# Expert weights of the fourth network: the split of all ten pieces moved ahead of the first chunk's mean, and cut in two parts

## The reference, cut to what matters

```
h = x @ W_in + b_in
for l in range(3):
    agg = segment_sum(h[src], dst) / deg
    logits = concat([h, agg]) @ router_W[l] + router_b[l]
    gates = softmax of the two largest logits, 0 elsewhere
    weak   = relu(agg @ weak_W[l]   + weak_b[l])          # 4 experts, 256 -> 256
    sh     = relu(agg @ strong_W1[l] + strong_b1[l])      # 4 experts, 256 -> 512
    strong = sh @ strong_W2[l] + strong_b2[l]             #            512 -> 256
    h = h + sigmoid(h @ conf_W[l] + conf_b[l]) * sum(gates * experts)
out = h @ W_out + b_out
```

## Time and profile before

| | us |
|---|---|
| median of the three runs | 3216.36 |
| profiled execution, its own time | 3218.61 |
| its span, first to last instruction | 3216.3 |
| fourth network's layers | about 1631 to 3181 of the span |
| mean granted TensorE clock | 0.975 |

### The profile page before, as it was taken

How to read it: one execution, slowest core, us unless ns; L and a number is a source line. 1 busy time by engine, 2 the same in 40 slices (tenths; PEclk the granted TensorE clock), 3 DMA queues, 4 the chain that set the end, 5 groups by cost and what they waited for, 6 DMA issues and landing times. The chain is left out here.

```text
span 3216.3 us, 47575 instructions
## 1 busy us (share of the span) xinstructions
PE 2951.0 (92%) x18761; PEld 1780.5 (55%) x18761; DVE 2189.7 (68%) x4024; ACT 914.5 (28%) x1695; POOL 18.1 (1%) x23
## 2 busy tenths in 40 slices
PE   2888889999988999999979999988999998999997
PEld 2566555555443545454545666654666664666665
DVE  7999555557227777776657767675767675676676
ACT  3788421114101000000032222233222233232222
POOL 2000000000000000000000000000000000000000
PEclk8899999999998999999989999999999999999999
DMA  5455366775006554544330000020000001000001
GB/s 127 139 151 150 110 192 210 223 230 165 22 9 184 157 171 150 182 145 127 88 106 3 4 3 4 3 82 4 4 7 4 3 27 60 3 4 3 4 3 42
DMA packets 310959, 265.85 MB, mean 83 GB/s; under 512 B 32767, under 2 KB 289409, under 8 KB 308174
## 3 DMA queue, kind: packets, MB, share of 16 engines
q1 hardware_dynamic: 296558, 259.28, 26.3%
q10 hardware_dynamic: 13760, 2.61, 0.4%
q0 software_dynamic: 416, 0.85, 0.1%
HBM read 172.67 MB, written 90.05 MB: 82 GB/s over the span
## 5 line engine op out<-in xcount | busy, mean ns | idle before, releaser
L1874 PE MATMUL psum<-r_wd,r_h 128*128 128x512 fp8e4 (+1 forms) x2600 | 568.4, 375 | 13.4 <-ACT r_h L229 12.9
L2483 PE MATMUL psum<-m_weights,x_nodes 128*128 128x256 f16 (+1 forms) x3600 | 419.7, 275 | 18.0 <-DVE m_wtmp L2267 16.4
L2464 PE MATMUL psum<-m_agg,m_weights 128*128 128x512 f16 (+2 forms) x2016 | 410.3, 356 | 21.7 <-ACT m_agg L2364 21.7
L2422 PE MATMUL psum<-counts,m_h 128*128 128x512 fp8e4 (+2 forms) x2100 | 417.6, 354 | 12.6 <-DVE m_h L2153 12.6
L1874 PEld LDWEIGHTS psum<-r_wd,r_h 128*128 128x128 f16 x2600 | 241.4, 97 | 307.5 <-issue 16.0
L2483 PEld LDWEIGHTS psum<-m_weights,x_nodes 128*128 128x128 f16 (+1 forms) x3600 | 353.7, 99 | 73.3 <-DVE m_wtmp L2267 16.5
L2422 PEld LDWEIGHTS psum<-counts,m_h 128*128 128x128 f16 x2100 | 206.2, 99 | 206.0 <-issue 18.8
L2364 ACT ACTIVATE m_agg<-psum,x_nodes 128x512 f32<-128x512 f32 (+2 forms) x336 | 238.2, 719 | 279.2 <-PE psum L2464 271.2
L2464 PEld LDWEIGHTS psum<-m_agg,m_weights 128*128 128x128 f16 x2016 | 194.9, 99 | 218.8 <-issue 32.7
L2376 ACT ACTIVATE m_hT<-m_hT,m_g 128x256 f32<-128x256 f32 x300 | 135.8, 502 | 552.4 <-DVE m_hT L2281 552.4
L2267 DVE SCALAR_TENSOR_TENSOR m_wtmp<-psum,x_nodes,m_bias 128x256 f32<-128x256 f32 (+1 forms) x300 | 144.9, 483 | 139.0 <-PE psum L2483 137.9
(11 more groups left out here) (312 smaller groups left out, 3328.3 us busy)
## 6 DMA issues: line engine op xcount, KB each, us to landing
r_wd<-packed_sym SPq DMA_DIRECT2D x120, 640.0 KB, 4.1
packed_counts<-strip SPq DMA_DIRECT2D x21, 1800.0 KB, 7.8
sym_blocks<-packed_counts SPq DMA_DIRECT2D x88, 384.0 KB, 4.4
packed_sym<-sym_blocks SPq DMA_DIRECT2D x84, 384.0 KB, 3.3
w_stage<-in_L_gnn_strong_W SPq DMA_DIRECT2D x12, 1024.0 KB, 6.6
m_weights<-in_L_gnn_strong_W SPq DMA_DIRECT2D x21, 512.0 KB, 4.7
x_parked<-x_nodes SPq DMA_DIRECT2D x2, 1600.0 KB, 5.9
x_nodes<-x_parked SPq DMA_DIRECT2D x2, 1600.0 KB, 6.5
```

What stands on the lines that cost most here:

```text
L1874: m = pe.matmul(bank[pair[b]][:, 0:2 * cw], h16[:, part, p0 + i, :], f_[:, 2 * b:2 * b + 2, :], start=(p0 + i == 0 and part == 0), stop=(p ...
L2422: m = pe.matmul(bank[kb][:, 0:cw], h16[:, part, i, kb * P:(kb + 1) * P], A[:, i, c_:c_ + cw], start=(i == 0 and part == 0), stop=(i == NT ...
L2464: m = pe.matmul(bank[4 + hh % 2][:, 0:cw], w_[:, i, kb, f * P:(f + 1) * P], agg16[:, j, kb, 0:cw], start=(x_ == 0), stop=(x_ == len(todo) ...
L2483: m = pe.matmul(bank[b_][0:r_, 0:H], s_[:, pa[0] * BANK + k * P:pa[0] * BANK + k * P + r_], w_[:, pa[1], f, :], start=(f == 0 and pa == PA ...
```

## The change

- `FIRST` goes; all ten pieces are split before `mean(0)`, on ACT as on DVE.
- Each piece is split in two parts of 512 columns (`HALVES`). ACT writes the high half of both parts with one wait ahead; DVE writes the low half of a part when ACT has done that part. ACT's wait for piece k asks for DVE's first part of piece k - 1 only: the high half of piece k lies over the first part of piece k - 1's float32 values.
- DVE's first part of a piece waits for its own previous piece (`w_low`).
- The scales' ten tiny instructions stand behind the splits, ahead of `mean(0)`.
- The semaphores' counts are doubled; TensorE's list is unchanged.

```
-                FIRST = 4
+                HALVES = (slice(0, SL // 2), slice(SL // 2, SL))
...
                     def split_low(k):
...
-                        vec.wait_ge(w_high, l * NPC + k + 1)
-                        vec.scalar_tensor_tensor(flat[:, 1, :], loaded_piece(k), scale_of(l, n_, wsc), flat[:, 0, :], ALU.mult,
-                                                 ALU.subtract).then_inc(w_low, 1)
+                        for x_, c_ in enumerate(HALVES):
+                            vec.wait_ge(w_high, 2 * (l * NPC + k) + x_ + 1)
+                            if k and x_ == 0:
+
+                                vec.wait_ge(w_low, 2 * (l * NPC + k))
+                            vec.scalar_tensor_tensor(flat[:, 1, c_], loaded_piece(k)[:, c_], scale_of(l, n_, wsc), flat[:, 0, c_], ALU.mult,
+                                                     ALU.subtract).then_inc(w_low, 1)
...
-                    for k in range(FIRST):
+                    for k in range(NPC):
                         split_low(k)
+                    vec.wait_ge(mrw_in, MRW_IN)
...
                     mean(0)
...
-                        if ci == 0:
-                            for k in range(FIRST, NPC):
-                                split_low(k)
                         weak(ci, ts[0:1])
...
                     def split_high(k):
...
                         if k:
-                            act.wait_ge(w_low, l * NPC + k)
-                        act.activation(flat[:, 0, :], loaded_piece(k), ACT.Copy, scale=scale_of(l, ORDER[k][0], wsc)).then_inc(w_high, 1)
+
+                            act.wait_ge(w_low, 2 * (l * NPC + k) - 1)
+                        for c_ in HALVES:
+                            act.activation(flat[:, 0, c_], loaded_piece(k)[:, c_], ACT.Copy, scale=scale_of(l, ORDER[k][0], wsc)).then_inc(w_high, 1)
...
-                    for k in range(FIRST):
+                    for k in range(NPC):
                         split_high(k)
                     turn(0)
...
-                        if ci == 0:
-                            for k in range(FIRST, NPC):
-                                split_high(k)
                         weak(ci, ts[0:1])
```

More of the change, by code:

```diff
@@ L2153, in dve_layer @@
                         vec.scalar_tensor_tensor(h16[:, 1, s, :], h2[:, s, :], sc[:, 1:2], h16[:, 0, s, :], ALU.mult, ALU.subtract).then_inc(e_low, 1)
[L2154 to L2167, removed]
                     def split_low(k):
@@ L2251, in hidden @@
                             if loc < NSH and loc >= NSH - 2:
-                                vec.wait_ge(w_low, (l + 1) * NPC)
+                                vec.wait_ge(w_low, 2 * (l + 1) * NPC)
                             if loc >= NSH:
@@ L2287, in weak @@
                                 vec.wait_ge(k_added, NWK * t + e + 1)
-                    for k in range(FIRST):
+                    for k in range(NPC):
                         split_low(k)
+                    vec.wait_ge(mrw_in, MRW_IN)
+                    if l == 0:
+                        vec.wait_ge(parked, 16)
+                    vec.tensor_scalar(ks[:, 0:1], sc[:, 0:1], float(H), wmax[:, l:l + 1], ALU.mult, ALU.mult).then_inc(steps.handle, steps.up())
+                    settle()
+                    vec.tensor_tensor(ks[:, 0:1], ks[:, 0:1], wmax[:, 3 * NLAY + l:3 * NLAY + l + 1], ALU.add).then_inc(steps.handle, steps.up())
+                    settle()
+                    power_scale(ks[:, 0:1], ks[:, 1:2], ks[:, 2:3], ks[:, 3:4])
+                    vec.tensor_scalar(k_hidden, ks[:, 1:2], sc[:, 2:3], w_inv["w1"], ALU.mult, ALU.mult).then_inc(steps.handle, steps.up())
+                    vec.tensor_tensor(k_strong, ks[:, 2:3], w_inv["w2"], ALU.mult).then_inc(steps.handle, steps.up())
+                    vec.tensor_tensor(k_weak, sc[:, 2:3], w_inv["ww"], ALU.mult).then_inc(steps.handle, steps.up())
+                    vec.tensor_scalar(b1s[:], b1[:, l], ks[:, 1:2], None, ALU.mult).then_inc(steps.handle, steps.up())
+                    settle()
+                    mark["h_bias", l] = steps.n
                     mean(0)
@@ L2455, in hidden @@
                         w_ = pair_of(PNO[("w1", e)], KB)
-                        pe.wait_ge(w_low, l * NPC + PNO[("w1", e)] + 1)
+                        pe.wait_ge(w_low, 2 * (l * NPC + PNO[("w1", e)] + 1))
                         pe.wait_ge(e_mean_low, l * NCH + ci + 1)
@@ L2469, in strong @@
                         w_ = pair_of(PNO[("w2", e)], FB)
-                        pe.wait_ge(w_low, l * NPC + PNO[("w2", e)] + 1)
+                        pe.wait_ge(w_low, 2 * (l * NPC + PNO[("w2", e)] + 1))
                         for i, k in tiles_of(CH[ci]) if tiles is None else tiles:
@@ L2493, in weak @@
                                 w_ = pair_of(PNO[("ww", pr)], KB)
-                                pe.wait_ge(w_low, l * NPC + PNO[("ww", pr)] + 1)
+                                pe.wait_ge(w_low, 2 * (l * NPC + PNO[("ww", pr)] + 1))
                                 pe.wait_ge(e_logits, l * NCH + ci + 1)
```

## The result

The changed kernel takes **3180.18 us** (median of 4 runs, 3177.92 to 3181.8); the kernel before, run beside it, 3217.44 us (4 runs, 3214.8 to 3218.89). The ratio is 0.9885, with a 95% interval of 0.9872 to 0.9897: 37.3 us saved. The forecast was 3178.9, with a range of 3175 to 3188. The profiled run took 3179.72 us, with a span of 3177.6 us and a mean granted clock of 0.977.

The account below looks back on a forecast made before the run. TensorE, busy 92%, was taken as the bound, with two stops in chunk 0 of each layer. Saving 12.74 + 12.47 + 12.47 = 37.68 us, less a 0.15 wait, gave -37.5: from the median 3216.36 to 3178.9 us, range 3175 to 3188.

Parts of the forecast that it names:

- The stops: TensorE's two idle times in chunk 0, layer 0: 4.58 us before the first `weak`, 4.88 before `strong`; removal saves 37.68 in all.
- a whole round: Saving taken from TensorE's next, stop-free round, 12.64 us from `weak` to `weak`, instead of adding up idle time.
- slow restart: TensorE running slower after a stop: 12 matmuls take 4.11 us instead of 2.75; rivals priced it at 1.4 per layer.
- the first stop: TensorE idle 4.58 us to 1684.54 in layer 0, said to wait for DVE's split of the second `ww` piece.
- The cycle: Time per piece on ACT and DVE: 0.754 + 0.724 + 0.13 for two handovers = 1.61 us, instead of 2.56.
- The chain and the mean: Ten splits, then scales, before `mean(0)`: first mean instruction ends 1660.71, TensorE wants it at 1660.60; about 0.15 us wait, layer 0.
- No overlap: Rival, 3%: the parts save nothing, cycle stays 2.56, each layer waits 8.6 us or a little less and pays 1.4; 3208.
- Parts in turn: Rival, 3%: every part waits for the one ahead, cycle 3.2, chain 15.3 us longer; 3229, slower than before.
- The turning point: Where the change becomes a loss: chain longer by over 11.2 us, a cycle of 2.8 and more.
- The mean late: Rival, 5%: cycle 2.0 under load, chain 3.5 us longer, waits of 3.7, 3.1 and 3.4 before `edges(1)`; 3189.
- The clock falls at a short wait: Rival, 2%: the small wait ahead of `edges(1)` brings the clock to 1.2 GHz, about 1.4 us per layer; 3183.

Follow-up runs that it names:

- parts in turn: Changed kernel with one more wait: ACT's second part of a piece waits for DVE's first part of the same piece; 3222.85 us, 1.0014 of the kernel before.
- the run with four additions: Changed kernel with four extra 512-column additions on DVE between the last piece's split and the scales; 3205.57 us, 0.9965 of the kernel before.
- the parts alone: Kernel before with each piece split in two parts, four pieces still ahead of the mean and six in chunk 0; 3198.02 us, ratio 0.9947.
- the place alone: Changed kernel with all ten pieces ahead of the mean, but each split whole (1024 columns); 3223.96 us, 1.0025 of the kernel before.
- six whole pieces ahead: Kernel before with six pieces instead of four split ahead of the mean, each whole; 3210.41 us, ratio 0.9978.
- the smaller first group: Changed kernel with the nodes split in groups of 2, 3 and then 5 tiles instead of 5 each; 3178.00 us, 0.9878 of the kernel before.
- both edits: Changed kernel with nodes split in groups of 2, 3, then 5 tiles and the scales moved behind the mean; 3174.65 us, 0.9868 of the kernel before.

## Why the prediction was right

**The number.** The forecast was a saving of 37.5 us, and 37.3 was measured. That the two are so close is in part luck: in the traces 37.75 us were saved at the forecast place, 1.2 were lost in the later chunks, and 2.15 came from a start that varies by several us from run to run. The mechanism is borne out apart from the number, by the rows below and by the variants.

**The stops.** The method of a whole round gave 12.74, 12.47 and 12.47 us; 12.68, 12.54 and 12.53 were measured (sum 37.68 and 37.75). Counting idle and slow restart one by one would have been less safe, as the next point shows.

**One reading of the profile was wrong.** The prediction said that the first stop waits for the second `ww` piece. It waited for the first, whose split ends at 1683.20 + 1.28 = 1684.48, and TensorE starts at 1684.54. The second ends at 1687.04, and TensorE's weight loads show a second wait inside the group of 12 matmuls (kernel before, layer 0; DVE's split of the first `ww` piece, then the loads):

```profile
1683.20 1.28 DVE L2173 SCALAR_TENSOR_TENSOR m_weights<-m_weights,m_wmax 128x1024 f16<-128x1024 f32 x1 [1.28 <-ACT m_weights L2328]
```

```profile
1686.22 0.15 PEld L2500 LDWEIGHTS psum<-m_weights,m_agg 128*128 128x128 f16 x1 [0.28 <-issue]
1687.10 0.13 PEld L2500 LDWEIGHTS psum<-m_weights,m_agg 128*128 128x128 f16 x2 [0.72 <-DVE m_weights L2173]
```

The loads before it stand 0.43 us apart, so the one at 1687.10 came 0.45 late. Of the 4.11 - 2.75 = 1.36 us that the prediction called the slow restart, 0.45 was this wait. The forecast isn't touched, since the round has both in it; the rivals are.

**The cycle.** 1.61 us was predicted from half durations of 0.754 and 0.724 and two handovers; 1.60 was measured, with a part of 0.72 on ACT (the single row of the variant with parts in turn). The straight line between 1024 and 768 columns was the right row to take, and not the two other ACT instructions of 512 columns (0.630, 0.814). The page "ScalarE: Activation LUTs" of the Trainium skill, section "What ACT_TABLE_LOAD costs", gave 0.706 as an estimate for the same part, 2% below. No engine slowed the other down, as the earlier trace rows had suggested.

**The chain and the mean.** The chain from the first split to its end took 15.84 us (15.91 predicted), and the first mean instruction ended 18.16 us after the chain's start (18.23 predicted). The wait in layer 0 was 0.11 where 0.15 was predicted, and none in the two others. The second mean instruction, the router and the scales that ACT needs were in time, as was every load. The first `weak` found DVE idle, 0.79 us.

**The rivals.** Four of them were tried by changing the kernel, and three come out otherwise than written. What failed in all three is the price of a slow restart: 1.4 us for each layer in two of them, nothing in the third.
- *No overlap* (cycle 2.56) was put at 3208, faster than before. Its waits were nearly right, its price was 5.5, 1.5 and 7.5 us; 3223.96 was measured, slower than before.
- *Parts in turn* was put at 3229 by a cycle of 3.2. The cycle was 2.40 and the price 7.4, 1.7 and 7.9; 3222.85 was measured. These are two errors of opposite sign. The turning point that the prediction gave, a cycle of 2.8, is wrong with it: at 2.40 and at 2.56 the kernel is already slower than before.
- *The mean late* at a cycle of 2.0 was put at 3189, with waits of 3.7, 3.1 and 3.4 us and no price at all. No run had that cycle or waits of just that size. The nearest is the run with four additions: in its profiled execution, 3196.91 us, the waits were 1.29, 2.62 and 2.28, and the last two cost 3.3 and 6.6 on top of themselves; its median is 3205.57. By the table above that rival would have paid about 1.5 to 7.9 us in each layer on top of its waits; this is an estimate.
- *The clock falls at a short wait*: it doesn't at 0.19 to 1.31 us, which is what the earlier trace rows said with its 0.80. The Trainium skill, page "TensorE: Matmul & The Clock Gate", section "A second HAM failure mode: psum-queue depth-cycling", speaks of small idles that come frequently between groups of matmuls. The prediction stretched that to a single short wait in each layer; no run here has the frequent ones, so the six waits without a fall neither bear the rule out nor go against it.

So the forecast stood on a chain that just makes it, 0.1 us late in layer 0. By the variants a wait of up to 1.3 us costs only itself. Beyond that the ground is steeper than the prediction had it: waits of 1.96, 2.28 and 2.62 us cost 8.6, 8.9 and 5.9 us each. That the gain is whole rests on place and cycle together: both save 37, the parts alone 18.5, and the place alone loses 7.4 (medians).

## What to carry to other kernels

Two engines that hand a piece back and forth can be made to overlap by cutting the piece in two, if the part that the one engine reads is not the one that the other writes; and the shorter cycle is what makes an earlier place for the work affordable. Look for the engine that stops, find the instruction queue that was late for it, and ask which work in that queue could have been done while the engine had a long group of its own, then work out, in the worst layer, whether the work still ends before its new deadline. A wait of TensorE of some 2 us cost two to four and a half times itself here, where small, loosely packed groups followed it; one of up to 1.3 us cost only itself.

## What the runs showed of the hardware

- **The lower clock lasts longer in loosely packed work.** Behind stops of 3.7 to 5 us ahead of 12 or 24 large matmuls the loss was 0.9 to 3.0 us (0.9 in the kernel before, worked out above; 2.5 with six whole pieces ahead: 1698.64 - 1693.54 = 5.10 against 2.62; 1.3 to 3.0 behind a stop of 3.8 to 4.1 us in the last chunk, which every kernel has in every layer and this change doesn't touch). Behind waits of 2 to 8 us ahead of the router, where groups of six alternate with 128x9 float32 matmuls, it was 1.5 to 7.9 us, and once (parts in turn, layer 2) the lower clock reached into `hidden(0, 0)`, whose 24 matmuls took 6.87 us instead of 5.34.
- **The clock also falls without any idle.** In chunks 3 and 5 the router's last tiles follow each other with nothing between them, and TensorE does only 128x9 matmuls for 2.6 us. In 30 of the 39 layers of the profiled runs the 24 matmuls behind them in chunk 5 take 6.9 to 7.03 us instead of 5.34, up to 1.69 more. TensorE, changed kernel, layer 1:

```profile
2518.62 0.59 PE L2447 MATMUL psum<-m_rw,m_agg 128*128 128x9 f32 x4
2519.07 0.59 PE L2447 MATMUL psum<-m_rw,m_hT 128*128 128x9 f32 x4
...
2520.41 0.59 PE L2447 MATMUL psum<-m_rw,m_agg 128*128 128x9 f32 x4
2520.85 7.03 PE L2463 MATMUL psum<-m_agg,m_weights 128*128 128x512 f16 x24
```

  It came in two of three layers before and after, though not in the same ones: layer 0 of the changed kernel has the same rows ahead and then 5.34. In the run with six whole pieces ahead it came six times, in chunks 3 and 5 of all three layers, and in the one with ten whole pieces five times: 6.4 and 4.8 us more than in the kernel before, none of it from the edit's own place. That is where part of the 12.5 us of the first of them went. In chunk 3 it came nine times in all, only in those two runs, with parts in turn and with the additions, and never in the kernel before or after. What decides it, whether an edit somewhere else can set this off, or whether it was chance, these runs don't settle. It also means that a difference of under 2 us between two kernels here may be one such event.
- **The start of `edges(0)` is at the lower clock.** In the kernel before the granted clock is 0.67 in layer 0 and 0.55 in layer 1 over its first 4 us. For the same 100 matmuls it took 22.9 to 24.4 us behind 4.2 us of idle (30 layers, 23.3 on average), 23.9 on average behind 2.8 us (6 layers) and 24.1 behind 2.3 (3 layers). So an earlier start is given back in part: of the 1.44 us that the smaller first group brought, 0.4 to 0.9 us was left with both edits. With the spread as large as this, single layers tell little.
